# Each batch's 64x64 output matrix on its own quarter of TensorE's array

## The reference, cut to what matters

```python
u   = ln_channels(x)                                  # over the 64 channels
qkv = Wqkv @ u + bqkv                                 # (192, 1024)
attn = softmax((q * 8**-0.5) @ k.T) per head          # 8 heads of 8x8: channel attention over the tokens
o   = attn @ v
x1  = x + Wout @ o + bout
t   = ln_tokens(x1.T)                                 # (1024, 64)
r   = softmax(softmax(mean(t) @ Wr + br) * scale)     # 8 experts, routed per batch
y   = sum over the top two experts of w_e * (gelu(t @ W1[e] + b1[e]) @ W2[e] + b2[e])
out = x1 + layer_norm(y + t) * gamma + beta
```

## Time and profile before

| | |
|---|---|
| runs | 118.45, 119.22, 122.53 us; median 119.22 |
| profiled execution, span from first to last instruction | 117.0 us (no other time of it is given) |
| PE busy | 94.2 us (80%), 626 instructions |
| DVE busy | 68.5 us (59%) |
| ACT busy | 50.1 us (43%) |
| POOL busy | 40.7 us (35%) |
| chain that ended last, by engine | PE 52%, DVE 18%, issue 8%, POOL 6%, DMA 5% |
| mean granted TensorE clock | 0.956 |

### The profile page before, as it was taken

How to read it: one execution, slowest core, us unless ns; L and a number is a source line. 1 busy time by engine, 2 the same in 40 slices (tenths; PEclk the granted TensorE clock), 3 DMA queues, 4 the chain that set the end, 5 groups by cost and what they waited for, 6 DMA issues and landing times.

```text
span 117.0 us, 2060 instructions
## 1 busy us (share of the span) xinstructions
PE 94.2 (80%) x626; PEld 46.6 (40%) x629; DVE 68.5 (59%) x276; ACT 50.1 (43%) x76; POOL 40.7 (35%) x93
## 2 busy tenths in 40 slices
PE   0059998989997999676599879999999998989300
PEld 0023497976763546344133223233342333234100
DVE  0299996723374188489869106835185273769850
ACT  0400504615325435407666592892983769050000
POOL 3000724900006000236801649940460550095190
PEclk9999999999999999999558999999999999999985
DMA  3999960000000000002583000560000030004124
GB/s 76 330 421 401 404 248 0 6 0 0 0 0 6 0 0 0 0 0 62 121 203 70 3 3 0 123 146 6 0 3 0 0 150 35 0 17 182 70 90 179
DMA packets 4314, 9.81 MB, mean 84 GB/s; under 512 B 592, under 2 KB 848, under 8 KB 4304
## 3 DMA queue, kind: packets, MB, share of 16 engines
q1 hardware_dynamic: 3728, 8.34, 21.6%
q10 hardware_dynamic: 576, 1.34, 3.2%
HBM read 5.49 MB, written 2.10 MB: 65 GB/s over the span
## 4 chain that ended last, share of the span: by engine, by line
PE 52%; DVE 18%; issue 8%; POOL 6%; DMA 5%; POOLq 5%; ACT 3%; ACTq 0%; DVEq 0%
PE pC L1080 10%; PE pC L886 6%; DMA cst<-consts_dram 5%; POOL XT L220 4%; PE pA L1053 4%; PE pM L956 4%; DVE UF L626 4%; PE pB L1053 4%; PE pS L827 3%; POOLq L437 3%; PE pA L837 3%; PE pM L891 2%; PE pB L949 2%; PE pC L973 2%; PE pS L891 2%
## 5 line engine op out<-in xcount | busy, mean ns | idle before, releaser
L1080 PE MATMUL pC<-H,w2g 128*64 128x512 f32 x64 | 15.8, 603 | 0.5 <-POOL w2g L452 0.5
L362 ACT ACTIVATE H<-pA,b1g 128x1024 f32<-128x1024 f32 x8 | 8.9, 1111 | 8.8 <-PE pA L1053 8.8
L535 DVE BATCH_NORM_STATS2 bst<-XT 128x6 f32<-128x64 f32 x64 | 9.4, 214 | 5.1 <-DMA XT<-x_tok_dram 5.1
L227 POOL TENSOR_TENSOR UT<-XT,rt 128x1024 f32<-128x1024 f32 x3 | 6.7, 2243 | 14.8 <-issue 10.9
L210 POOL CAST R<-r 128x16 bf16<-128x16 f32 (+1 forms) x5 | 1.0, 203 | 29.2 <-DVE r L525 29.2
L220 POOL TENSOR_TENSOR XT<-XT,T 128x512 f32<-128x512 f32 x7 | 9.2, 1334 | 4.0 <-DVE XT L788 4.0
L956 PE MATMUL pM<-cst 128*128 128x480 f32 x6 | 4.6, 904 | 7.2 <-DMA cst<-consts_dram 7.2
L753 DVE TENSOR_TENSOR c<-b2g 64x1 f32<-64x1 f32 x8 | 5.7, 716 | 5.9 <-POOL w2g L452 5.8
L966 PE MATMUL pB<-cstb 128*128 128x512 bf16 x27 | 8.8, 489 | 0.2 <-issue 0.2
L362 ACT ACTIVATE H<-pB,b1g 128x1024 f32<-128x1024 f32 x8 | 8.9, 1117 | 0.0
L419 POOL TENSOR_TENSOR LO<-UF,HI 128x1024 f16<-128x1024 f32 x4 | 8.4, 2128 | 1.2 <-ACT HI L308 1.2
(11 more groups left out here) (193 smaller groups left out, 177.1 us busy)
## 6 DMA issues: line engine op xcount, KB each, us to landing
X<-x_cha_dram SPq DMA_DIRECT2D x4, 512.0 KB, 11.3
out_dram<-XT SPq DMA_DIRECT2D x8, 256.0 KB, 2.0
XT<-x_tok_dram SPq DMA_DIRECT2D x3, 512.0 KB, 7.8
ST<-HI SPq DMA_DIRECT2D x8, 128.0 KB, 2.4
ST<-LO SPq DMA_DIRECT2D x8, 128.0 KB, 2.4
w_sb<-w_dram ACTq DMA_DIRECT2D x1, 512.0 KB, 8.1
cstb<-constb_dram ACTq DMA_DIRECT2D x1, 304.0 KB, 9.7
XT<-x_tok_dram ACTq DMA_DIRECT2D x1, 256.0 KB, 4.5
```

What stands on the lines that cost most here:

```text
L227: engine.tensor_tensor(UT[:, p, :, 1:P + 1].rearrange("p j (b c) -> p j b c", b=2), XT[:, p, :].rearrange("p (j b c) -> p j b c", b=2, c=C ...
L362: nc.scalar.activation(H[:, step % 2, b, :], h_ps[b][:, :], ACT.Gelu, bias=b1g[:, p % 2, b, k:k + 1], scale=1.0 / (S_U * S_W)).then_inc(s[ ...
L535: return nc.vector.bn_stats(bst[:, p // 2, i % (2 * G2), :], XT[:, p, g * C:(g + 1) * C])
L1080: last = mm(half(y_ps[:, cols], b), w2g[:, p % 2, b, k, :], H[:, step % 2, b, cols], start=False, stop=(k == TOP - 1))
```

## The change

Rows and columns trade places in one half of the kernel. M_b is no longer put on the diagonal of a 128x128 tile: `MTs[:, p, :]` holds the two 64x64 matrices one above the other, and `conv(p)` is four 64x64 matmuls. The one for batch b and token half h reads array rows of batch b and writes array columns of half h. A pair's result so lies with partition = 64*(token half) + channel and columns = (batch, 512 tokens). T, UF, ZS, OUT and x keep this layout; x is loaded and the output stored in transfers of 128 partitions by 512 tokens, one per batch. What was per pair on the partitions and is now per batch gets its own column: biases `cbs` and `c2`, and the sums `su`, so that `normal2` becomes two instructions of 512 columns. The bias product takes a two-column block layout of `bv` (`bvbd`). The router weights come straight from PSUM (`ps_wr`, a copy of them that a matmul with the identity makes), since each of the 128 partitions now needs the same 8 values for every batch. Two POOL clears and two POOL copies go.

```diff
-        MTs = sb("MTs", [P, NP, P])
-        cbs = sb("cbs", [P, NP])
+        MTs = sb("MTs", [P, NP, C])
+        bvbd = sb("bvbd", [P, 2])
+        cbs = sb("cbs", [P, B])
-        su = sb("su", [P, NP])
-        wrbd = sb("wrbd", [P, 2 * E])
+        su = sb("su", [P, B])
-        c2 = sb("c2", [P, NP])
+        c2 = sb("c2", [P, B])
-        ps_lg = pS[:, 0:B * E]
+        ps_lg, ps_wr = pS[:, 0:B * E], pS[:, B * E:B * E + E]
...
             for p in range(NP):
-                sp.dma_start(X[:, p, :], x_cha[:, p, :]).then_inc(s_x[p], 16)
+                for b in range(2):
+                    sp.dma_start(X[:, p, b * HALF:(b + 1) * HALF],
+                                 x_cha[b * C:(b + 1) * C, p, :].rearrange("c (h n) -> h c n", h=2)
+                                 ).then_inc(s_x[p], 16)
...
-                    for b in range(2):
-                        sp.dma_start(ST[half * C:(half + 1) * C, 2 * p + b, :],
-                                     src[b * C:(b + 1) * C, p, :]).then_inc(s_st[p], 16)
+                    for h in range(2):
+                        sp.dma_start(ST[half * C:(half + 1) * C, 2 * p:2 * p + 2, h * HALF:(h + 1) * HALF],
+                                     src[h * C:(h + 1) * C, p, :].rearrange("c (b n) -> c b n", b=2)
+                                     ).then_inc(s_st[p], 16)
...
             def evac_mt(g):
                 act.wait_ge(s["mt"], g + 1)
-                act.wait_ge(s["clear"], 1)
-                for b in range(2):
-                    rows = slice(b * C, (b + 1) * C)
-                    last = nc.scalar.copy(MTs[rows, 2 * g:2 * g + 2, rows], ps_mt[g][rows, :, :])
-                last.then_inc(s["mts"], 1)
+                nc.scalar.copy(MTs[:, 2 * g:2 * g + 2, :], ps_mt[g]).then_inc(s["mts"], 1)
...
             nc.scalar.copy(wvc[:, :], pS[:, 300:300 + C]).then_inc(s["wcv"], 1)
+            act.wait_ge(s["bvz"], 1)
+            act.wait_ge(s_wsm, 16)
+            for b in range(2):
+                nc.scalar.copy(bvbd[b * C:(b + 1) * C, b:b + 1], w("bv", b * C, (b + 1) * C)).then_inc(s["bvd"], 1)
...
-            nc.gpsimd.memset(MTs[:, :, :], 0.0).then_inc(s["clear"], 1)
+            nc.gpsimd.memset(bvbd[:, :], 0.0).then_inc(s["bvz"], 1)
...
-            nc.gpsimd.memset(wrbd[:, :], 0.0).then_inc(s["onesm"], 1)
-            pool.wait_ge(s["onesm"], 2)
             scale1(1)
             scale1(2)
             scale1(3)
-            pool.wait_ge(s["wcv"], 1)
-            for b in range(2):
-                rows = slice(b * C, (b + 1) * C)
-                nc.gpsimd.tensor_copy(wrbd[rows, b * E:(b + 1) * E], wTc[rows, WR]).then_inc(s["wrb"], 1)
-                pool.wait_ge(s["wrb"], b + 1)
...
             def normal2(p):
                 dve.wait_ge(s["rb"], p + 1)
-                nc.vector.scalar_tensor_tensor(out=UF[:, p, :], in0=T[:, p, :], scalar=1.0, in1=rb[p % 2][:, :],
-                                               op0=ALU.mult, op1=ALU.mult,
-                                               accum_out=su[:, p:p + 1]).then_inc(s["uf"], 1)
+                for b in range(2):
+                    cols, i = slice(b * HALF, (b + 1) * HALF), 2 * p + b
+                    nc.vector.scalar_tensor_tensor(out=UF[:, p, cols], in0=T[:, p, cols], scalar=1.0,
+                                                   in1=rb[p % 2][:, cols], op0=ALU.mult, op1=ALU.mult,
+                                                   accum_out=su[:, i:i + 1]).then_inc(s["uf"], 1)
...
-            dve.wait_ge(s["uf"], NP)
-            dve.wait_ge(s["wrb"], 2)
-            nc.vector.tensor_tensor(sw[:, :].rearrange("p (l e) -> p l e", l=NP),
-                                    wrbd[:, :].unsqueeze(1).broadcast_to([P, NP, 2 * E]),
-                                    su[:, :].unsqueeze(2).broadcast_to([P, NP, 2 * E]), ALU.mult).then_inc(s["sw"], 1)
+            dve.wait_ge(s["wrp"], 1)
+            dve.wait_ge(s["uf"], B)
+            nc.vector.tensor_tensor(sw[:, :].rearrange("p (b e) -> p b e", b=B),
+                                    ps_wr.unsqueeze(1).broadcast_to([P, B, E]),
+                                    su[:, :].unsqueeze(2).broadcast_to([P, B, E]), ALU.mult).then_inc(s["sw"], 1)
...
                         mm(half(ps_mt[g][:, l, :], b), half(wvc[:, :], b), half(B1s[:, g, l, :], b),
                            start=True, stop=True)
-                        last = mm(half(ps_cb[g][:, l:l + 1], b), half(B1s[:, g, l, :], b), half(w("bv"), b),
+                pe.wait_ge(s["bvd"], 2)
+                for l in range(2):
+                    for h in range(2):
+                        last = mm(half(ps_cb[g][:, 2 * l:2 * l + 2], h), B1s[:, g, l, :], bvbd[:, :],
                                   start=True, stop=True)
...
-                for h in range(2):
+                for b in range(2):
                     if p >= 1:
-                        pe.wait_ge(s["t"], 2 * p + h - 1)
-                    cols = slice(h * HALF, (h + 1) * HALF)
-                    mm(cv[:, cols], MTs[:, p, :], U[:, p, cols], start=True, stop=True).then_inc(s["conv"], 1)
+                        pe.wait_ge(s["t"], 2 * p + b - 1)
+                    for h in range(2):
+                        last = mm(half(cv[:, b * HALF:(b + 1) * HALF], h), half(MTs[:, p, :], b),
+                                  half(U[:, p, h * HALF:(h + 1) * HALF], b), start=True, stop=True)
+                    last.then_inc(s["conv"], 1)
...
             keep_awake(5)
+            pe.wait_ge(s["red2"], NP)
+            mm(ps_wr, cf("ident"), wTc[:, WR], start=True, stop=True).then_inc(s["wrp"], 1)
             turn2(1)
```

More of the change, by code:

```diff
@@ L198, in build_program @@
         s_out = [sem(f"s_out{p}") for p in range(NP)]
-        names = ("ones clear onesm wrb sw wcp wcv gram gs tb u p1 p1s s_ps sms exs a_sb b1 b1s mt mts cbs conv t "
+        names = ("ones onesm wrp sw bvz bvd wcp wcv gram gs tb u p1 p1s s_ps sms exs a_sb b1 b1s mt mts cbs conv t "
                  "row rw mom pow1 pow2 red2 r3 rt rr rb uf hi lo w1p w1h w1l w2p w2v lg rexp1 rexp2 "
@@ L416, in low @@
             def low(p):
[L417 removed]
+                pool.wait_ge(s["uf"], 2 * p + 2)
                 pool.wait_ge(s["hi"], p + 1)
@@ L587, in att_bias, with residual1 @@
                 dve.wait_ge(s["mts"], g + 1)
-                nc.vector.tensor_tensor(cbs[:, 2 * g:2 * g + 2], w("bout").broadcast_to([P, 2]), ps_cb[g],
+                nc.vector.tensor_tensor(cbs[:, 4 * g:4 * g + 4], w("bout").broadcast_to([P, 4]), ps_cb[g],
                                         ALU.add).then_inc(s["cbs"], 1)
-            def residual1(p, halves=(0, 1)):
+            def residual1(p, batches=(0, 1)):
                 dve.wait_ge(s["cbs"], p // 2 + 1)
[L593 to L597, removed]
+                dve.wait_ge(s_x[p], 32)
+                for b in batches:
+                    cols, i = slice(b * HALF, (b + 1) * HALF), 2 * p + b
+                    dve.wait_ge(s["conv"], i + 1)
+                    nc.vector.scalar_tensor_tensor(out=T[:, p, cols], in0=cv[:, cols], scalar=cbs[:, i:i + 1],
                                                    in1=X[:, p, cols], op0=ALU.add, op1=ALU.add).then_inc(s["t"], 1)
@@ L751, in bias2 @@
                 for b in range(2):
-                    rows = slice(b * C, (b + 1) * C)
-                    last = nc.vector.tensor_tensor(c2[rows, p:p + 1], b2g[rows, p % 2, b, 0:1],
-                                                   b2g[rows, p % 2, b, 1:2], ALU.add)
+                    last = nc.vector.tensor_tensor(c2[:, 2 * p + b:2 * p + b + 1], b2g[:, p % 2, b, 0:1],
+                                                   b2g[:, p % 2, b, 1:2], ALU.add)
                 last.then_inc(s["c2d"], 1)
@@ L759, in evac_z @@
                 dve.wait_ge(s["mm2"], TOP * (p + 1))
[L760 to L761 removed]
+                for b in range(2):
+                    if b:
                         dve.wait_ge(s["sq3"], 2 * p + 1)
[L763 to L764 removed]
+                    cols, i = slice(b * HALF, (b + 1) * HALF), 2 * p + b
+                    nc.vector.tensor_scalar(ZS[:, p, cols], y_ps[:, cols], c2[:, i:i + 1], w("gamma"),
                                             ALU.add, ALU.mult).then_inc(s["zs"], 1)
@@ L1065, in residual3 @@
                 pe.wait_ge(s_st[p], 64)
-                for h in range(2):
-                    cols = slice(h * HALF, (h + 1) * HALF)
-                    for b in range(2):
-                        mm(half(y_ps[:, cols], b), cb("cenr"), ST[:, 2 * p + b, cols], start=True, stop=False)
+                for b in range(2):
+                    for h in range(2):
+                        mm(half(y_ps[:, b * HALF:(b + 1) * HALF], h), cb("cenr"),
+                           ST[:, 2 * p + b, h * HALF:(h + 1) * HALF], start=True, stop=False)
             def down(step, between=None):
@@ L1076, in down @@
                 pe.wait_ge(s["g2"], 2 * (step + 1))
-                for h in range(2):
```

(9 more changed lines are left out.)

22 lines of the change are left out of this document (12 added, 10 removed).

## The result

The changed kernel took 151.0 us (median of 6 runs, 150.39 to 151.90), the kernel before 118.84 (6 runs, 118.22 to 122.53) on the same chip. The ratio is 1.270, 95% interval 1.264 to 1.276: 32 us slower, where 2 us faster was forecast.

A forecast was written before the change was run, and what follows sets the result against it. It took the chain of waits (52% PE, else DVE) as the bound, then TensorE's clock. Terms -1.28 (conv to conv(2)), +0.40 (normal2) and -1.18 (sw) gave -2.06 us, from the median 119.22 to 117.2 us, range 114.6 to 119.9.

The forecast's parts named there:

- At nothing: List of changes costed at zero, among them the x loads in eight transfers, the output stores, and removed POOL work.
- conv to conv(2): First conv to third: four quarter-array matmuls at once and one matrix copy; L562 1.12 us earlier, conv(2) 1.28 us earlier.
- Rivals 3: In conv, quarters of one column group take turns, so it keeps 1.72 us; total -0.6, 118.6 us; chance 0.14.
- 4 (strict order of the passes): In conv, each quarter's second pass waits for its first, 2.15 us per conv; total +0.8, 120.0 us; chance 0.04.
- normal2: Second normalization: four instructions of 1024 columns become eight of 512, three pairs on the path; +0.4 us (0 to 1.1).
- sw: DVE product before the logits: with one operand in PSUM 0.24 us instead of 1.42 beside POOL's LO; -1.18 us.
- The sum of these, -2.06: Whole kernel: -1.28 up to conv(2), +0.40 for normal2, -1.18 for sw; span from 117.0 to 114.9 us.
- Rival 1: TensorE's clock doesn't fall, or only briefly, so keep_awake(18) takes 1.9 us less; 115.3 us; chance 0.16.
- Rival 2: TensorE's clock falls earlier, ahead of conv(3), and returns later, behind keep_awake(18); total +2.5, 121.8 us; chance 0.08.

The follow-up runs named there:

- e1: Changed kernel with x laid in DRAM as (token half, channel), so loads are 128 even rows, output stored as in the changed kernel; ratio 1.160, 137.8 us.
- e2: Changed kernel with the output laid in DRAM as (token half, channel), so stores are 128 even rows, x as in the changed kernel; ratio 1.092, 129.7 us.
- e3: Changed kernel with both x and output laid in DRAM as (token half, channel); ratio 0.980 to the kernel before, runs of 115.87 and 117.01 us.
- e8: e3's kernel with conv as four matmuls of 128 rows by 64 columns, zeros in the other batch's rows, and two matrix copies again; 118.70 and 119.13 us.
- e7: e3's kernel with sw reading the router weights from SBUF instead of PSUM; 121.16 us in one run.
- e11: Kernel before with one part of the change alone, sw's second operand read from PSUM; ratio 0.987, runs of 116.99 to 118.33 us.
- e9: e3's kernel run again, in more rounds; ratio 0.983 to the kernel before, runs of 115.91 to 117.08 us.
- e4: Changed kernel, DRAM layout as it was, each x load and output store split into two of 64 rows, one per token half; ratio 1.002.
- e5: e3's kernel with gap rows in x's DRAM layout, making the outermost dimension 16, 8, 4, 2 for pairs 0 to 3; 120.79 us in one run.
- e10: e3's kernel with keep_awake(12) instead of keep_awake(18) behind the logits; runs of 116.17 and 116.23 us.

## Why the prediction was wrong

**The step that failed** is one half-paragraph, "At nothing". It said of x: "x comes in eight transfers instead of four, all issued behind the tokens and weights; DMA is silent from 18 us on, and the first x is used at 28.45, so 10 us cover it", and of the output: "Bytes of the output and their last transfer are the same." It counted bytes, pieces and issues, and asked for no rate; the old form of the transfer ran at some 400 GB/s (397 from 10 to 15 us of before). The new one ran at 50, since a 2 had become the outermost dimension. Ten microseconds of cover would have been ample for eight transfers at 400 GB/s (5 us), and cannot cover 42. The range 114.6 to 119.9 had no rival for it: all five were about PE and its clock. What e1, e2 and e3 measured for the step is +13 us for x, +21 for the output, +34 in all, where the sum had 0.

**conv to conv(2): right.** Four quarters ran at once (1.09 us in the trace of the changed kernel), vbs (L562 before) and `conv(2)` came 1.29 and 1.35 us earlier relative to `conv(0)` in e3, where 1.12 and 1.28 were summed from the old start of `conv(0)`, that is 1.22 and 1.38 relative to it. e8 shows that it is the quarters that bring it at vbs (6.49 without them, 4.90 with them), and they and the single copy at `conv(2)`. One step of the working doesn't add up: 27.29 + 0.86 + 0.1 puts `gram(3)` at 28.25, where 28.35 is written; the trace has it 1.02 us behind `conv(0)`, between the two. Rivals 3 (quarters of a column group take turns) and 4 (strict order of the passes) are both refuted by the eight MATMULs in 1.09 us.

**normal2: right in sign, too high.** +0.08 per pair, 0.24 on the path; 0.4 was summed, with bounds of 0 and 1.1.

**sw: right.** 0.23 for the 0.24 forecast; e7 (both operands in SBUF: 0.84, done 0.09 behind LO) and e11 (one in PSUM: 0.22, with LO running on to 59.02) show it from both sides.

**The sum of these, -2.06, holds once the transfers are repaired:** e9's 0.983 of 118.86 is 2.0 us less, e3's 0.980 is 2.4 less. How much of it is from these steps can't be told to better than about 1 us, since where the clock falls and returns differs by trace (e11: 4.62 us for the same eighteen matmuls; e4: 6.47), so that the total meets the forecast this closely is in part luck. Rival 1's shorter low stretch was there in e3, e8 and e11 (3.4 us instead of 6.8); in e11 it gave `keep_awake(18)` 1.3 us, most of which was lost again by the last `down`. Rival 2's early fall was there in the changed kernel, from 45.6 to 66.1 us. PE had been busy for 2.03 of the 4.6 us before it, while DVE waited for x; that this brought the fall was not tested.

## What to carry to other kernels

When a change rearranges a transfer, read the new access pattern's outermost dimension before its bytes: if no even stride covers the rows, the 2 of a "(h n) -> h c n" may be all the engines it gets, 50 GB/s instead of 400 as in the changed kernel here. Two transfers of 64 rows take the loss away (e4), but nothing of the gain was left in e4's runs, 1.5 us of it for the further issues at the end; a layout in DRAM that makes the rows even kept it (e3), with the reordering done on the host, outside the measured time. And in a list of things "at nothing", each cover needs a duration from a row of the same form of transfer: here no row had an outermost dimension of 2, so its cost should have been bounded and not put at nothing.

## What the runs showed that was not expected

- The number of busy DMA engines followed the outermost dimension, 2.2, 4.2, 7.5 to 8.2 and all 16 by the shares, and the rate less than in proportion: 51 GB/s at 2, 96 at 4, 151 to 170 at 8, 271 at 16 (e5).
- A slow transfer held SP: seven issues of 256 KB took 31 us, where all eight took 5.27 in e3. Nothing urgent stood behind them in that queue here; what would have, would have waited.
- One DVE product of 64 columns whose operands both lie in SBUF ended 0.1 us behind POOL's instruction each time: it took 1.41 us before, 0.84 in e7, and 0.23 with one operand in PSUM.
- TensorE's low stretch in the middle, with a granted clock of 0.50, was 55.4 to 62.2 us in the trace of before, about the same in e4, but 56.2 to 59.6 in e8 and e11, and 62.5 to 65.9 in e10, over the first expert steps. The same kernel has 57.6 to 61.0 in e3 and 53.0 to 63.3 in e9, and the end of its last `down` lies 72.54 and 73.33 us behind `conv(0)`, 0.8 apart. What places the stretch is not settled. At a granted clock of 1.00 `keep_awake`'s matmuls of 512 bf16 columns start 0.215 us apart (before, two of them from 35.91 to 36.34), at 0.50 they start 0.43 us apart (58.55 and 58.98), so 2.4 and 1.2 columns per ns: these are the 2.4 and 1.2 GHz of the forecast.
- Matmuls on all four quarters, each pair sharing rows or columns, ran as one in `conv`: 8 passes in 1.09 us (changed kernel and e3), about two slots of 0.43 and the end of the last.
